# Projection to q, k and v: GpSimd applies the layer norm with two operations over a whole block, in place of four instructions of ScalarE

## The reference

```python
def _layernorm(x, axis=-1, eps=1e-05):
    m = jnp.mean(x, axis=axis, keepdims=True)
    v = jnp.var(x, axis=axis, keepdims=True)
    return (x - m) / jnp.sqrt(v + eps)
...
x = x + 0.5 * _L0_ffn_ref(_layernorm(x, axis=-1), ...)
x = x + _L0_attn_ref(_layernorm(x, axis=-1), ...)
...
qkv = jnp.einsum('btc,fc->btf', x, w_qkv)
```

## Time and profile before

| | before |
|---|---|
| median of 3 runs | 1820.78 us (1819.0 to 1821.32) |
| the profiled execution | 1819.8 us |
| its span, first to last instruction | 1818.0 us |
| PE, DVE busy in it | 1670.5 us (92%), 1294.9 us (71%) |
| ACT, POOL busy in it | 1093.9 us (60%), 860.1 us (47%) |

### The profile page before, as it was taken

How to read it: one execution, slowest core, us unless ns; L and a number is a source line. 1 busy time by engine, 2 the same in 40 slices (tenths; PEclk the granted TensorE clock), 3 DMA queues, 4 the chain that set the end, 5 groups by cost and what they waited for, 6 DMA issues and landing times. The chain is left out here.

```text
span 1818.0 us, 33373 instructions
## 1 busy us (share of the span) xinstructions
PE 1670.5 (92%) x11129; PEld 1160.4 (64%) x11176; DVE 1294.9 (71%) x2826; ACT 1093.9 (60%) x1612; POOL 860.1 (47%) x656
## 2 busy tenths in 40 slices
PE   7999787989889889897999799998899999899998
PEld 7888673333333333337888677776677777777776
DVE  5454895777777777775546598876787787768886
ACT  3332688999999999993333222223888887722120
POOL 0002107999999999994003232211256565411111
PEclk9999898999999999999999899999999999999999
DMA  5000275634535536400001000000322233200000
GB/s 161 1 0 12 70 210 99 83 51 64 75 46 72 66 46 82 57 2 0 12 1 35 24 7 0 0 0 15 101 99 94 93 117 106 94 1 24 23 23 24
DMA packets 57095, 95.07 MB, mean 52 GB/s; under 512 B 7888, under 2 KB 29616, under 8 KB 57008
## 3 DMA queue, kind: packets, MB, share of 16 engines
q1 hardware_dynamic: 56048, 93.35, 23.7%
q10 hardware_dynamic: 960, 0.59, 0.1%
HBM read 76.88 MB, written 17.04 MB: 52 GB/s over the span
## 5 line engine op out<-in xcount | busy, mean ns | idle before, releaser
L1456 POOL TENSOR_TENSOR att_weights<-att_weights 128x1024 f32<-128x1024 f32 (+1 forms) x288 | 508.9, 1799 | 8.6 <-DVE att_weights L1393 5.3
L1393 DVE SCALAR_TENSOR_TENSOR att_weights<-att_weights,ps 128x512 f32<-128x512 f32 x544 | 348.0, 683 | 144.8 <-ACT att_weights L1362 138.2
L894 DVE SCALAR_TENSOR_TENSOR X<-ps,moe_gsel,X 128x256 f32 (+1 forms) x512 | 246.5, 483 | 63.1 <-PE ps L48 47.1
L1317 PE MATMUL ps<-att_weights,att_v_ones 64*32 64x64 f32 (+5 forms) x2048 | 289.0, 399 | 1.9 <-POOL att_weights L1456 1.8
L1362 ACT ACTIVATE att_weights<-att_weights 128x1024 f32<-128x1024 f32 (+1 forms) x288 | 286.5, 1007 | 1.0
L1356 ACT ACTIVATE att_weights<-ps 128x1024 f32<-128x1024 f32 (+1 forms) x288 | 278.5, 973 | 8.2 <-PE ps L1297 7.0
L48 PE MATMUL ps<-w_experts_hi,moe_xh 128*128 128x512 f32 x512 | 205.2, 401 | 0.4 <-DVE X L894 0.4
L48 PE MATMUL ps<-w_experts_hi,moe_xl 128*128 128x512 f32 x512 | 203.1, 397 | 0.0
L48 PE MATMUL ps<-w_experts_lo,moe_xh 128*128 128x512 f32 x512 | 201.6, 394 | 0.0
L1317 PEld LDWEIGHTS ps<-att_weights,att_v_ones 128*32 128x32 f32 (+1 forms) x2048 | 82.3, 108 | 104.7 <-issue 80.3
L412 ACT ACTIVATE ffn_gates<-ps,ffn_gate_bias 128x512 f32<-128x512 f32 x72 | 49.6, 689 | 151.8 <-PE ps L48 145.3
(11 more groups left out here) (283 smaller groups left out, 3802.1 us busy)
## 6 DMA issues: line engine op xcount, KB each, us to landing
ssm_lb<-decays SPq DMA_DIRECT2D x32, 512.0 KB, 4.7
ssm_rise<-decays SPq DMA_DIRECT2D x28, 512.0 KB, 3.8
qk_parts<-qkv_part SPq DMA_DIRECT2D x32, 384.0 KB, 2.9
q_stack<-qk_parts SPq DMA_DIRECT2D x64, 128.0 KB, 4.7
k_stack<-qk_parts SPq DMA_DIRECT2D x64, 128.0 KB, 8.6
att_q_stack<-qk_parts SPq DMA_DIRECT2D x64, 128.0 KB, 4.8
att_k_stack<-qk_parts SPq DMA_DIRECT2D x64, 128.0 KB, 8.7
out<-X SPq DMA_DIRECT2D x8, 512.0 KB, 2.9
```

Source lines behind the costliest of these rows:

```text
L894: dve.scalar_tensor_tensor(out=x, in0=ring[:, e // 2, (e % 2) * C:(e % 2 + 1) * C], scalar=gsel[:, s, j, e:e + 1], in1=x, op0=ALU.mult, op ...
L1317: ins = pe.matmul(O(qb)[h * 2 * HD:(h + 1) * 2 * HD, q0:q0 + w], values, Wt[rows, u % WU, t, c:c + w], start=kj == 0 and part == FULL, sto ...
L1393: dve.scalar_tensor_tensor(out=wt[:, t], in0=wt[:, t], scalar=LIMIT, in1=scores(u)[:, t], op0=ALU.min, op1=ALU.max).then_inc(max_done, 2 // n)
L1456: pool.tensor_tensor(wt, wt, wt, ALU.mult).then_inc(sq_pool, 1)
```

## The change

ACT's four activations are taken out of step n, and out of the preamble (where they were for group 1). POOL does the same with two operations over the 128x1024 block, first `X` minus the mean, then times the root; mean and root are one value per token and are held over the 256 columns of a tile. The second waits for the first through a new semaphore `shifted`. POOL also waits for the turn of the group that used the same `xn` before (`turned`), and in the preamble for DVE's apply of group 0. `shift` and its two small operations are gone. DVE's wait ahead of its steps asks for the root in place of `shift`.

```diff
--- before.py
+++ after.py
@@ -1027,7 +1027,7 @@
         ring = ps[:, 2:2 + RING]
         unit_done, v_done, v_read = sem("unit_done"), sem("v_done"), sem("v_read")
         part0_done, part1_done, part2_done = sem("part0_done"), sem("part1_done"), sem("part2_done")
-        rest_done = sem("rest_done")
+        rest_done, shifted = sem("rest_done"), sem("shifted")
         tail.open(sem)
         stored = [sem(f"stored{h}") for h in range(HALVES)]
         block = ctx.enter_context(nc.Block())
@@ -1086,8 +1086,6 @@
                     first(n, h, u)
                     if u < QK - 1:
                         second(n, h, u - 1)
-                if left >= 2:
-                    norm.act_apply(act, n + 2, h, lambda j: tile_of(n + 2, j))
                 for u in range(QK - 2, QK):
                     second(n, h, u)
                 if left >= 3:
@@ -1104,7 +1102,6 @@
             tail.act_tanh(act, 1)
             norm.act_hi(act, 0, 0)
             tail.act_tanh(act, 2)
-            norm.act_apply(act, 1, 1, lambda j: tile_of(1, j))
             steps(act, step)
 
         @block.vector
@@ -1151,17 +1148,30 @@
             norm.dve_stats(dve, 1, 1, lambda j: tile_of(1, j))
             tail.dve_add(dve, 2, 0)
             norm.dve_lo(dve, 0, 0)
-            dve.wait_ge(norm.shift_done, 1)
+            dve.wait_ge(norm.rstd_done, 1)
             steps(dve, step)
 
         @block.gpsimd
         def _(pool):
+            def apply(n, s):
+
+                norm.pool_rstd(pool, n, s)
+                pool.wait_ge(norm.rstd_done, n + 1)
+                if not isinstance(n, int) or n > 1:
+                    pool.wait_ge(norm.turned, n - 1)
+                x = X[:, bass.ds(n * GW, GW)].rearrange("p (t c) -> p t c", t=GT)
+                xn = norm.xn[s][:, :].rearrange("p (t c) -> p t c", t=GT)
+                pool.tensor_tensor(xn, x, norm.mv[:, s, :, 0:1].broadcast_to([P, GT, C]), ALU.subtract).then_inc(shifted, 1)
+                pool.wait_ge(shifted, n)
+                pool.tensor_tensor(xn, xn, norm.rstd[:, s].unsqueeze(2).broadcast_to([P, GT, C]), ALU.mult).then_inc(norm.xn_done, 1)
+
             norm.pool_setup(pool)
-            norm.pool_shift(pool, 0, 0)
-            norm.pool_shift(pool, 1, 1)
+            norm.pool_rstd(pool, 0, 0)
+            pool.wait_ge(norm.xn_done, 1)
+            apply(1, 1)
             with pool.Fori(0, GROUPS // 2 - 1) as i:
                 for h in range(HALVES):
-                    norm.pool_shift(pool, i * 2 + 2 + h, h)
+                    apply(i * 2 + 2 + h, h)
 
         @block.sync
         def _(sp):
```

## The result

| | before | after |
|---|---|---|
| median of 5 runs each | 1820.78 us (1819.0 to 1822.78) | 1830.74 us (1828.41 to 1830.93) |
| the profiled execution, its span | 1819.8, 1818.0 us | 1828.41, 1826.6 us |

The ratio is 1.0050, with a 95% interval of 1.0036 to 1.0065: slower by 10 us. The forecast was 1830.1 us.

What follows compares the result with a forecast made beforehand. DVE was taken to bound the qkv phase at 10.96 us per group. Groups 5.8, start 2.6 and clock 0.9 sum to 9.3 us over the median of 1820.8, so 1830.1 us, range 1826 to 1837.

Steps and rivals of the forecast that it cites:

- The clock term: At the last turn: PE's wait grows to 2.9 us, its clock may fall and the turn slow down, 0.9 us.
- The price of a POOL operation: Each new 128x1024 subtract or multiply on POOL takes 1.89 us, between bounds of 1.70 and 2.39.
- the rival with 2.39: POOL's operations cost 2.39 us like those with two full tensors: 1837 at most, chance 15%.
- The hold-up in a group: DVE's two-SBUF-input operations wait for POOL's: 1.44 us per group, 5.8 us over groups 3 to 6.
- The start: Start of the qkv phase: second turn 2.15 us later, first L1114 1.4 us more, less 0.95 given back: 2.6 us.
- The end: From the last power to its turn and PE's work behind it: no change counted.
- "DVE is the bound": In the qkv phase DVE, without idle brackets, sets the 10.96 us per group through groups 2 to 6.
- "Taking 2.06 us from ACT brings nothing by itself": Per group, removing ACT's apply of 2.06 us gains nothing; what counts is what POOL's new work does to DVE.
- No hold-up: Rival: the hold-up doesn't occur for these shapes, DVE keeps 10.96 us per group: 1821 us, chance 8%.
- Less hold-up: Rival: DVE is held for less, half the holds in groups and start: 1826.5 us, chance 6%.
- PE's waits as the bound: Rival: PE's waits before its turns set the pace, so up to 6 us faster, to 1815 us, chance 2%.
- A hold of POOL by the wait for `turned`: Rival: the new wait could hold POOL; dismissed, as it asks for a turn a group back; no chance given.

Runs made afterwards that it cites:

- e1: Kernel before, ACT's apply kept, plus the change's two POOL operations per group into a block nobody reads: 1833.81 us, ratio 1.0076.
- e7: Kernel before, ACT's apply kept, plus two POOL memsets of 128x1792 per group into memory nobody reads: 1821.09 us, ratio 1.0004.
- e9: Kernel after, with 9 unread identity matmuls on PE in front of the turns of groups 1 and 3: 1831.89 us, ratio 1.0041.
- e10: Kernel before, ACT's apply cut to one of four tiles for groups 2 to 7 (wrong values): 1820.23 us, ratio 0.9991.
- e4: Kernel after, with the apply of group 1 given back to ACT: 1828.19 us, ratio 1.0038.
- e3: Kernel before, DVE's third parts reading one tensor, the second part's subtraction left out (wrong values): 1820.32 us, ratio 1.0001.
- e11: Kernel before, with ACT's apply cut as in e10 and DVE's third parts lightened as in e3: 1817.39 us, ratio 0.9971.
- e2: Kernel after, DVE's third parts reading one tensor, the second part's subtraction left out (wrong values): 1829.27 us, ratio 1.0051.
- e12: Kernel after, with group 1's apply on ACT and each POOL operation cut into two of 128x512: 1826.79 us, ratio 1.0026.
- e6: Kernel after, with each of POOL's two operations cut into two of 128x512: 1829.61 us, ratio 1.0048.

## Why the prediction was right

The sign and the mechanism held: 9.3 us forecast, 9.74 in the phase and 9.96 between the medians. That the sum came so near is partly luck. The clock term of 0.9 us did not occur; without it the forecast would have been 8.4, and the other terms were 1.34 us short: 0.78 in the groups, 0.24 at the start, 0.32 at the end. Its steps one by one:

- **The price of a POOL operation**, 1.89 us: 1.90. By the measured 1.90 us the estimate of 2.25 us from the Trainium skill, page "GPSIMD Engine Reference", section "3.1 Elementwise — side-by-side cycle accounting", is too high for an operand that is held over 256 columns; the rival with 2.39 falls with it.
- **The hold-up in a group**, 1.44 us: 1.59 to 1.78 in the rows, a mean of 1.66, and 1.65 in the distance, so the term 5.8 should have been 6.6. What was mis-sized is mostly the release. I took 0.20 us before POOL's recorded end, from one pair of rows; it is 0.14 at the first third and 0.13 at the second, which makes 0.13 of the 0.15 us in the group worked through. Behind the `qkv_var` of groups 4 and 6 the first third is held longer, 0.77 and 0.87: POOL's subtract starts 1.53 and 1.52 us behind `qkv_var` instead of 1.45, and behind group 6's the third asks 0.11 us sooner. e1 shows that the POOL operations alone do it, e7 that being busy and writing is not enough.
- **The start**, 2.6 us: 2.84. Two steps in it were off and cancel. The second turn was 2.10 us late, as forecast (2.15), but at half the clock, so L170 was 2.97 late and not 2.15. The first third was then held by 0.17 and not by more than a microsecond. In truth both lead to the same end of the multiply: the third really started 3.60 us late (3.43 and 0.17), where the forecast had 3.55. e9 shows the forecast's way, with the hold in full. Given back were 0.76 of the 0.95 us; e10 has 0.79.
- **The end**, 0: +0.32. From the last `qkv_var` to its turn it is 5.70 us, and was 5.67, and from that turn to the end of PE's products for q and k it is the same 13.33 us. The other 0.29 us stands in ACT's idle time before the table load (3.68, before 3.39), and why is not shown.
- **The clock**, 0.9 us at the last turn: 0 in after, so this term was wrong. PE's waits did not grow to 2.9 us: they are 1.86, 1.94, 2.14 and 1.33 us before the last four turns. The step that failed is the one that laid the hold on top of PE's wait: from `qkv_var` to turn a group takes 5.70 us, no more than before, and the added time lies elsewhere in the group. The granted clock fell in after behind 2.61 and 2.14 us of waiting and not behind 1.86, 1.94 and 1.33; in e4 it fell behind 2.06, at the last turn, and the end was 1.24 us longer there than in after. A fall at that turn was thus possible, and that after had none is chance as far as these runs tell.
- **"DVE is the bound"** was half of the truth. Rows without an idle bracket show that DVE is never idle; they don't show that a shorter DVE would help. "ACT is not: it ... has time left" is wrong: e3, e10 and e11 show a tie with the loop through ACT. For time added to DVE this makes no difference, and so the forecast didn't suffer. **"Taking 2.06 us from ACT brings nothing by itself"** holds per group (e10: 10.97), for this reason.
- **The rivals.** No hold-up: excluded by every row above. Less hold-up: it was more. PE's waits as the bound: the wait is 1.94 now and DVE still sets the pace. A cost by late delivery of `xn`, which the prediction didn't list, is out too: e1, where POOL delivers nothing new, costs 12 us. A hold of POOL by the wait for `turned`: no row of POOL in after waits for PE.

The end of e2, 0.52 us shorter than that of before, has two parts: the last turn comes 5.44 us behind its `qkv_var` instead of 5.67, since the lighter third part holds POOL's multiply for less, and ACT's idle time before the table load is 3.11 instead of 3.39, as in e3 (3.10). Still open: the 0.29 us at the end of after, and whether the clock's fall at the last turn in e4 comes each time; e4 has one profiled execution, and its slowest.

## What to carry to other kernels

Before work goes to GpSimd, look at what VectorE does in the same microseconds: with SBUF reads on both sides they can shut each other out, in some operations even where VectorE has one input only, and GpSimd's free time is then no free time. The price is not GpSimd's duration but what is left of its operation when VectorE's next such operation wants to start; work it out row by row, and prefer short GpSimd operations, or place them beside VectorE operations that read PSUM. And an engine without idle time is a bound for what you add, but only an experiment that shortens it tells whether it is one for what you take away.

## What the runs showed of the hardware

- DVE and POOL shut each other out also where DVE's TENSOR_SCALAR reads a single f32 tensor from SBUF: 128x512 to bf16 took 0.42 us alone and 1.10 and 1.32 beside POOL, a 128x4 operation 1.77 instead of 0.17. BATCH_NORM_STATS2 reads a single f32 tensor too and was not held: four took 1.40 us beside POOL's multiply in after (198.83), and 1.40 or 1.41 elsewhere.
- DVE's third parts get on 0.13 to 0.15 us before POOL's record ends. POOL's memsets (128x1792, 1.60 us) don't hold DVE.
- The length of a POOL operation with two inputs depends on the second: 1.90 us for 128x1024 with one value per 256 columns, 2.39 with two full tensors.
- The length of PE's wait alone doesn't tell whether the clock falls. It fell behind a wait of 1.89 us in e4 (0.55 over the next 2.7 us, so 1.2 GHz for nearly all of them), and stayed at 1.00 behind one of 3.24 us in e12. The two turns with their waits, and the granted clock in the us behind them, e4 first:

```profile
231.76 1.23 PE L151 MATMUL ps<-ident,ahead_xn 128*128 128x128 f32 x8 [1.89 <-POOL ahead_xn L1167]
```

```profile
232.30:235.00 2.70, 2.70 (x12) 2.22 (x10) 2.64 (x4) 1.31 (x2) 0.00 (x0) 0.55 0.44 118
```

```profile
256.25 1.09 PE L151 MATMUL ps<-ident,ahead_xn 128*128 128x128 f32 x8 [3.24 <-POOL ahead_xn L1171]
```

```profile
257.30:260.00 2.70, 2.70 (x13) 2.15 (x12) 2.59 (x6) 2.06 (x4) 0.00 (x0) 1.00 0.80 270
```

- Nor does the place: the turn at 245.65 in after, behind a wait of 1.94 us, took 1.09 us at 1.00. The same turn in e9, behind the same wait, took 1.93 us at a granted clock of 0.52, and the group took 12.55 us in both:

```profile
247.40 1.93 PE L151 MATMUL ps<-ident,qkv_xn 128*128 128x128 f32 x8 [1.94 <-POOL qkv_xn L1169]
```

- A turn at 1.2 GHz took 1.97 us, and cost nothing where the next engine would have been held anyway (after against e9, and the groups of e4 and e9 that kept their length). In e6, at the start, the low clock behind the turn made DVE wait.
